# Head attention: two calls of values one behind the other, in every second key tile

## What is computed

```python
# target, source: (B, 256, 512); 16 heads of 16 channels; the 512 columns are the positions
q = einsum('oc,bct->bot', Wq, target) + bq[None, :, None]
k = einsum('oc,bcs->bos', Wk, source) + bk[None, :, None]
v = einsum('oc,bcs->bos', Wv, source) + bv[None, :, None]
dot = einsum('bhdt,bhds->bhts', q, k) / sqrt(16)
mask = target_mask[:, :, :, None] * source_mask[:, :, None, :]
dot = mask * dot - (1.0 - mask) * 1e6
amap = softmax(dot, axis=-1) * mask
out = einsum('bhts,bhds->bhdt', amap, v)
```

## Time and profile before

| | us |
|---|---|
| runs, median of 3 | 1461.63 (1460.28 to 1463.44) |
| profiled execution, device time | 1464.9 |
| its span, first to last instruction | 1463.1 |
| head attention, first column product to last call of values | about 193 to 691 |

### The profile page before, as it was taken

One profiled execution on the slowest core, in us unless ns is written; L12 is line 12 of the kernel. 1 busy time (PEld: TensorE's weight loads), 2 busy tenths in 40 slices (PEclk: granted clock), 3 DMA queues, 4 the chain that ended last, 5 costly groups with the idle time before them and its releaser, 6 DMA issues.

```text
span 1463.1 us, 22978 instructions
## 1 busy us (share of the span) xinstructions
PE 1333.5 (91%) x8985; PEld 764.0 (52%) x9014; DVE 999.3 (68%) x1517; ACT 649.9 (44%) x941; POOL 224.8 (15%) x424
## 2 busy tenths in 40 slices
PE   5798878898988889987999999999999999999998
PEld 2344422222222223222767767776777777777776
DVE  8989578778787887785586856743457545475353
ACT  4677447777777777785263111122111321112210
POOL 2013133434334243321000000000000000000000
PEclk9999979999999999996999999999999999999999
DMA  6302212332334232231743311000020000111000
GB/s 191 114 18 63 74 50 70 116 97 76 104 93 132 84 102 70 88 105 58 257 154 119 105 63 58 2 30 1 23 66 1 30 1 1 53 35 30 2 1 30
DMA packets 78037, 101.21 MB, mean 69 GB/s; under 512 B 14679, under 2 KB 51647, under 8 KB 77927
## 3 DMA queue, kind: packets, MB, share of 16 engines
q1 hardware_dynamic: 75879, 99.43, 21.6%
q0 software_dynamic: 2048, 0.27, 0.1%
HBM read 78.07 MB, written 21.34 MB: 68 GB/s over the span
## 4 chain that ended last, share of the span: by engine, by line
PE 40%; DVE 8%; DMA 1%; issue 1%; ACT 1%; POOL 1%; POOLq 0%; DVEq 0%; SPq 0%; ACTq 0%
PE double L1743 13%; PE double L1757 11%; PE double L1769 6%; PE double L1822 3%; PE double L1790 3%; PE double L1779 3%; PE double L1809 1%; PE double L1727 1%; DVE stats L1930 1%; DMA x_early<-scr_x 1%; DVE hid L1977 1%; DVE gate L1975 1%; DVE x_early L1946 1%; DMA out_x<-x_early 1%; POOL rstd L1916 1%
## 5 line engine op out<-in xcount | busy, mean ns | idle before, releaser
L1019 ACT ACTIVATE prob<-level,head_scale 128x512 f32<-128x512 f32 x512 | 319.6, 681 | 94.4 <-PE level L935 92.9
L1333 DVE TENSOR_REDUCE nmx<-level 128x2 f32<-128x1024 f32 x256 | 305.2, 1220 | 77.9 <-PE level L925 77.9
L1855 ACT ACTIVATE th<-double 128x512 f32<-128x512 f32 x96 | 53.9, 561 | 384.4 <-PE double L1743 222.7
L935 PE MATMUL level<-stacks 59*128 59x512 f16 x512 | 176.3, 392 | 25.2 <-ACT prob L1019 25.2
L925 PE MATMUL level<-stacks 57*128 57x512 f16 x512 | 149.9, 396 | 11.3 <-DVE nmx L1333 10.6
L1743 PE MATMUL double<-x_parts,f0w 128*128 128x256 f16 x1408 | 156.6, 274 | 1.6 <-PEq L519 1.6
L1743 PE MATMUL double<-x_parts,f1w 128*128 128x256 f16 x1408 | 155.2, 273 | 0.0
L372 PE MATMUL level<-prob,x_parts 128*128 128x448 bf16 (+1 forms) x527 | 121.1, 383 | 31.8 <-ACT prob L324 17.2
L935 PEld LDWEIGHTS level<-stacks 59*128 59x128 f16 x512 | 40.5, 93 | 209.6 <-ACT prob L1019 166.7
L1743 PEld LDWEIGHTS double<-x_parts,f0w 128*128 128x128 bf16 x1408 | 138.4, 98 | 20.4 <-issue 2.3
L1743 PEld LDWEIGHTS double<-x_parts,f1w 128*128 128x128 bf16 x1408 | 137.5, 98 | 18.1 <-issue 0.3
(11 more groups left out here) (235 smaller groups left out, 1824.6 us busy)
## 6 DMA issues: line engine op xcount, KB each, us to landing
stacks<-scr_q SPq DMA_DIRECT2D x64, 96.0 KB
stacks<-scr_k SPq DMA_DIRECT2D x64, 96.0 KB
hid<-in_f1w1t SPq DMA_DIRECT2D x8, 704.0 KB, 6.3
hid<-in_f1w2t SPq DMA_DIRECT2D x8, 704.0 KB, 4.3
inputs<-in_x SPq DMA_DIRECT2D x8, 512.0 KB, 7.3
scr_q<-splits SPq DMA_DIRECT2D x16, 256.0 KB, 2.4
scr_k<-splits SPq DMA_DIRECT2D x16, 256.0 KB, 2.1
xres<-in_x SPq DMA_DIRECT2D x8, 512.0 KB, 6.6
```

The costliest lines, as they stand in the source:

```text
L935: nc.tensor.matmul(pB[n % 2], Ks[rows, g, j // 2, P * c:P * (c + 1)], Qs[rows, g, j // 2, :], start=True, stop=True).then_inc(s["b_pe"], 1)
L1019: nc.scalar.activation(prob[:, c, j, :], pB[(64 * b + 16 * g + 4 * c + j) % 2], ACT.Exp, scale=hscale[:, 5:6]).then_inc(s["exp_done"], 1)
L1333: nc.vector.tensor_reduce(nmx[:, g % 2, :, half, tt], pA[(32 * b + 8 * g + u // 2) % 2], AX.X, ALU.max, negate=True).then_inc(s["max_done" ...
L1855: y = nc.scalar.activation(th[:, 0:m, :], src[:, 0:m, 0:S], ACT.Tanh, scale=0.5 / XS)
```

## The change

Within a group, `values` is no longer called once in every key tile. At c = 2 the products for tiles 0 and 1 stand one behind the other, and at c = 0 of the next group those for tiles 2 and 3. At c = 1 and c = 3 there is none. Behind the last sequence two calls stand in place of one. Nothing else in the program is touched.

```diff
@@ -972,13 +972,16 @@
                             column_scores(b, g, c, 2 * half + 1)
-                            if half == 1:
-                                if c:
-                                    values(b, g, c - 1)
-                                elif g:
-                                    values(b, g - 1, DK - 1)
-                                elif not first:
-                                    values(b - 1, NG - 1, DK - 1)
+
+                            if half == 1 and c == 2:
+                                values(b, g, 0)
+                                values(b, g, 1)
+                            elif half == 1 and c == 0 and g:
+                                values(b, g - 1, 2)
+                                values(b, g - 1, 3)
+                            elif half == 1 and c == 0 and not first:
+                                values(b - 1, NG - 1, 2)
+                                values(b - 1, NG - 1, 3)
                             if present(jobs[half], first, last):
@@ -986,7 +989,8 @@
             over_sequences(body)
-            values(B - 1, NG - 1, DK - 1)
+            values(B - 1, NG - 1, 2)
+            values(B - 1, NG - 1, 3)
             run("t", 3, B - 1)
```

## The result

The changed kernel takes 1532.35 us (median of 4 runs, 1525.43 to 1541.16) against 1461.92 before: a ratio of 1.0485, 95% interval 1.043 to 1.0541, so 70 us slower. The profiled execution has 1533.18 us and a span of 1531.4. Note the spread of the runs, 16 us where the kernel before has 3 (and 9 over all its runs here): something in it is not fixed by the program alone.

A forecast was written before the change was run, and what follows sets the result against it. The prediction took a loop through PE and ACT, with two score buffers, to bound the head attention's slots. Order +27 and clock falls +40 gave +67, 1529 us against a median of 1461.6; range 1482 to 1575.

The forecast's parts named there:

- The order, +27: Head attention: moving the calls costs +3.37 us a sequence at full clock, +27 us over eight sequences.
- The second call: Slots with two calls (c = 0, 2): the added call lies wholly on the path, 0.91 us each.
- the floor of a bare slot: Slots without a call (c = 1, 3): the wait for the third exponential keeps them at 2.33 us.
- the 1.0 us of PE waits: Each slot: two score buffers tie column products to exponentials, leaving about 1.0 us of waits no reordering of values removes.
- The gain of (0,3): Group 0, key tile 3: its end follows a DVE chain that starts earlier as seen from the slot, -0.91 us.
- The clock, +40: Head attention: sparser stretches without calls make PE's clock fall to half, 21 falls at 1.9 us, +40 us.
- a third: Head attention: of 64 possible clock falls about this share, 21, was taken to happen.
- the upper bound: Price of one clock fall at a double call: 1.9 us taken, at most 2.8.
- No falls (1489): Rival: the clock holds throughout the head attention, so only +27 us, 1489 us; chance 0.20.
- Clock low for half the stage (1627): Rival: the head attention's clock stays low half the time, +138 us, 1627 us; chance 0.06.
- Faster, because PE is the bound: Rival: slots without a call give back all 1.00 us and tiling switches are saved, 12 us, 1450 us; chance 0.07.

The follow-up runs named there:

- experiment 2: Changed kernel plus 1 to 3 extra matmuls at places of slots without a call where PE waits, buffer wait only in front of them: 1495.22 us.
- Experiments 5 to 7: Changed kernel, paired calls parted across slot halves: 1504.76 us; kernel before, calls of four slots, then of (3,0) alone, in the first half: 1467.59 and 1458.83 us.
- experiments 3 and 4: Changed kernel with only tiles 0 and 1 paired: 1507.36 us; with only tiles 2 and 3 paired: 1490.9 us.

## Why the prediction was right

Forecast 1529, measured 1532: the sum has two terms, and both were near what the runs give. Their mechanisms are shown, by the slots at full clock and by experiment 2; that they add up to within 3 us is partly luck, as told below.

*The order, +27.* At full clock a sequence costs 3.1 more, +25; experiment 2 gives 2.9, +23. The slots, forecast and median at full clock: (0,2) 3.97 and 3.92; (2,0) 3.97 and 3.90; (1,3) 2.33 and 2.42; (0,1) 3.60 and 3.59; (0,3) 3.47 and 3.57; (2,1) 3.26 and 3.25; (2,3) 5.30 and 5.31; (0,0) 7.16 and 7.03; (1,0) 7.41 and 7.36. The second call was worth 0.86 and not 0.91, and the floor of a bare slot is 0.09 higher. The step behind it holds: where ACT has run out, a call is paid in full, and where PE waits for an exponential, it was paid in part only.

*A premise that was wrong.* The prediction says that no reordering of values removes any of the 1.0 us of PE waits in a slot. Experiments 5 to 7 do remove some: with its call in the first half, (3,0) lasts 2.70 in place of 3.06. The sum doesn't suffer, since the change itself moves no call into such a wait.

*A step that was misplaced.* The gain of (0,3) was ascribed to its being bare in part; experiments 3 and 4 show that the full slot ahead brings it. With both pairs in place the sum is the same, so only the halves were predicted wrong.

*The clock, +40.* Measured about 45, from 23 falls before the last sequence at about 2.0; forecast 21 at 1.9. The count was an estimate of "a third" and might have been off by a factor of two; that it hit is partly luck. The price hit for other reasons than those given: it was worked out as what a double call loses, 1.9, and that is 1.63 here; the score products and side jobs of the slot, which were not in it, lose about 1.0 more, and where the clock rises in the middle of the double call less is lost. So (0,2) and its like take 3.92 at full clock and up to 6.69 with a fall, +2.8, which was the upper bound, and the mean is 2.0.

*The rivals.* No falls (1489): excluded by the profile and turned into a measurement by experiment 2. The rule of the Trainium skill (TensorE: Matmul & The Clock Gate, Part 1) that an idle window lets the clock drop, read as a single long idle time, would have kept it at 1.00. The trace does not agree with that reading: PE was busy 1.96 of 3.59 in (0,1) by the profile, the fall came at the end of that slot, and the longest idle time of PE from 200 to 660 us was 1.12. The same part also tells of a kernel whose short idle times between groups of matmuls sufficed to make the clock swing, which I had passed over; this trace agrees with that. Clock low for half the stage (1627): about 22%. Faster, because PE is the bound: the bare slots gave 0.50 on average, far below the 0.95 needed; the switch of tiling is worth what the 1.85 against 2 x 0.99 shows, 0.13 a pair, 8 us in all, and the second call's 0.86 has it in already.

*The spread.* The changed kernel's runs differ by 16 us with one program, and go with their mean clocks: 1525.43 at 0.949, 1531.51 and 1533.18 at 0.945, 1541.16 at 0.935. So the program doesn't fix how long the clock stays low.

## What to carry to other kernels

Bundling work on the busiest engine did not help here, because that engine waits in every slot; in a loop through two engines with two buffers, first cut the trace into its steps and ask which wait each piece fills, since a piece that fills a wait is nearly free and the same piece one place later is paid in full. Price the clock as a resource of its own: in this kernel evenly spread matmuls held full speed, and the same matmuls in lumps lost it. And count a gained slot only after looking at the queue of the engine that comes next, as (2,1) and (0,0) showed.

## What the runs showed that I had not expected

Adding matmuls made a kernel 37 us faster (1532 to 1495), by the clock alone. Four calls a sequence, moved by half a slot, set off 4 falls of the clock in a stage that had none; the one call of (3,0) set off none. After an exponential's end the next slot's first column product started after 0.14 us in a bare slot (2.42 in place of 2.33), where within the slot the step is 0.06; why is open. Also open is what exactly makes the clock fall: the runs show where it falls and that extra matmuls there prevent it, not by what measure.
